# Cross-attention on one core: the last 26 keys as a fifth block of 32 instead of a transposition by TensorE

## The reference

```python
q = _split_heads(hidden_states @ Wq.T, H)
k = _split_heads(text @ Wk.T, H)
v = _split_heads(text @ Wv.T, H)
out_text = _merge_heads(_attend(q, k, v, sm_scale))
k_ip = _split_heads(ip @ Wk_ip.T, H)
v_ip = _split_heads(ip @ Wv_ip.T, H)
out_ip = _merge_heads(_attend(q, k_ip, v_ip, sm_scale))
out = out_text + IP_SCALE * out_ip
out = out @ Wo.T + bo
return out + residual
```

## Time and profile before

| | |
|---|---|
| median of 3 runs | 549.65 us (548.14 to 549.90) |
| the profiled execution | 547.71 us, span 545.7 us |
| TensorE busy | 517.2 us, 95% of the span |
| TensorE weight loads | 451.1 us, 83% |
| VectorE busy | 400.9 us, 73% |
| ScalarE busy | 386.0 us, 71% |
| GpSimd busy | 309.9 us, 57% |
| DMA | 130.13 MB, 78.8% of 16 engines' span, mean 238 GB/s |
| granted clock of TensorE, mean | 0.987 |

### The profile page before, as it was taken

The page is one execution under the profiler, slowest core; times in us unless marked ns, Lnnn a source line. Parts: engine busy times, 40 slices in busy tenths (PEclk is TensorE's granted clock), DMA queues, the critical chain, the costliest instruction groups (busy, mean ns, idle before and its releaser), DMA issues.

```text
span 545.7 us, 15177 instructions
## 1 busy us (share of the span) xinstructions
PE 517.2 (95%) x4994; PEld 451.1 (83%) x4994; DVE 400.9 (73%) x655; ACT 386.0 (71%) x1714; POOL 309.9 (57%) x343
## 2 busy tenths in 40 slices
PE   8999777899999999999999999999999999999897
PEld 8999666688887888888887888887888888888685
DVE  0024598988787888878887878887888878888822
ACT  0145578787877787878877887877887878877720
POOL 1032536566665848666747666666748566756530
PEclk9999878999999999999999999999999999999999
DMA  8992166877978787979788878888798979878772
GB/s 287 412 385 118 40 198 193 260 222 201 308 216 280 215 264 237 276 212 281 228 259 228 260 231 252 262 240 259 215 272 230 272 218 276 233 229 229 231 220 88
DMA packets 87005, 130.13 MB, mean 238 GB/s; under 512 B 9792, under 2 KB 71872, under 8 KB 86720
## 3 DMA queue, kind: packets, MB, share of 16 engines
q1 hardware_dynamic: 86976, 129.75, 78.8%
HBM read 77.29 MB, written 52.43 MB: 238 GB/s over the span
## 4 chain that ended last, share of the span: by engine, by line
PE 50%; issue 12%; POOL 11%; DMA 9%; DVE 7%; SPq 5%; ACT 5%; POOLq 0%; DVEq 0%; ACTq 0%
PE q_ps L633 13%; PE x_ps L633 13%; DMA p_main<-bounce_d 8%; POOL probs L343 6%; PE s_ps L658 5%; PE pv_ps L682 5%; PE pv_ps L679 4%; SPq L288 4%; PE s_ps L771 3%; ACT probs L406 3%; POOL res L368 2%; DVE row_neg L534 2%; PE pv_ps L771 2%; DVE turned L553 2%; POOL rest L349 2%
## 5 line engine op out<-in xcount | busy, mean ns | idle before, releaser
L343 POOL TENSOR_TENSOR probs<-probs,row_inv 128x616 f32<-128x616 f32 (+1 forms) x160 | 165.4, 1054 | 165.9 <-DVE row_inv L565 165.9
L406 ACT ACTIVATE probs<-s_ps,row_neg 128x77 f32<-128x77 f32 x640 | 197.9, 338 | 63.5 <-DVE row_neg L534 63.4
L534 DVE TENSOR_REDUCE row_neg<-s_ps 128x8 f32<-128x616 f32 x160 | 120.4, 794 | 34.4 <-PE s_ps L658 34.0
L406 ACT ACTIVATION_READ_ACCUMULATOR probs<-s_ps,row_neg 128x1 f32 x640 | 139.7, 218 | 0.0
L553 DVE STREAM_TRANSPOSE turned<-probs 128x512 f32<-128x512 f32 x160 | 103.9, 686 | 2.9 <-POOL probs L343 2.7
L560 DVE TENSOR_REDUCE row_sum<-probs 128x8 f32<-128x616 f32 x80 | 63.6, 795 | 42.6 <-ACT probs L413 42.6
L633 PE MATMUL q_ps<-x_hi,wq_hi 128*128 128x256 f32 x400 | 90.0, 324 | 0.0
L633 PE MATMUL x_ps<-attn_hi,wo_hi 128*128 128x256 f32 x375 | 75.4, 299 | 1.1 <-ACT y L431 1.1
L633 PE MATMUL q_ps<-x_hi,wq_lo 128*128 128x256 f32 x400 | 74.7, 285 | 0.0
L633 PE MATMUL q_ps<-x_lo,wq_hi 128*128 128x256 f32 x400 | 74.4, 284 | 0.0
L334 POOL TENSOR_TENSOR x_lo<-x_raw,x_hi 128x1280 fp32r<-128x1280 f32 x16 | 48.8, 3049 | 44.1 <-ACT x_hi L424 44.1
(11 more groups left out here) (72 smaller groups left out, 756.4 us busy)
## 6 DMA issues: line engine op xcount, KB each, us to landing
bounce_d<-turned SPq DMA_DIRECT2D x80, 512.0 KB, 3.0
p_main<-bounce_d SPq DMA_DIRECT2D x320, 128.0 KB, 3.5
x_raw<-x_in SPq DMA_DIRECT2D x16, 640.0 KB, 6.4
res<-x_in SPq DMA_DIRECT2D x75, 128.0 KB, 3.3
y_out<-res SPq DMA_DIRECT2D x75, 128.0 KB, 3.0
stage<-wk_in SPq DMA_DIRECT2D x6, 640.0 KB, 8.3
stage<-wv_in SPq DMA_DIRECT2D x6, 640.0 KB, 11.1
wq_raw<-wq_in SPq DMA_DIRECT2D x1, 1600.0 KB, 10.3
```

The costliest lines, as they stand in the source:

```text
L343: nc.gpsimd.tensor_tensor(rows[:, :, keys], rows[:, :, keys], row_inv[:, u.slot, :, br].unsqueeze(2) .broadcast_to([P, GROUP * SUB, size]) ...
L406: done = nc.scalar.activation(rows[:, cols], s_ps[:, j, cols], ACT.Exp, bias=row_neg[:, j, i:i + 1], accum_out=row_sum[:, j, i:i + 1])
L534: nc.vector.tensor_reduce(row_neg[:, heads_of(half)], by_row(s_ps[:, heads_of(half), 0:SUB * BLK]), AXIS.X, ALU.max, negate=True).then_inc ...
```

## The change

The last 26 keys take the way of the others, as a fifth block of 32. The probabilities get 64 zero columns at the end of each place, so that VectorE's second transposition may read past the last head's keys; it now does three blocks (the six rows beyond the 26 carry other heads' numbers and aren't loaded). The write to DRAM grows by a quarter, a fifth load brings 26 partitions into `p_last`, whose other rows stay zero, and TensorE does four more column products over it. `normalise_rest`, `turn_rest`, `keep_rest`, `head_rows` and `rest_of_values` go. The values of the last keys are transposed straight from `v_chan`, which is zero behind them.

Beside this `p_main` goes from five places to two and with `p_last` is protected by `pv_ready`, now one semaphore a place; SyncE issues three of a unit's loads before the next unit's write and two behind it; ScalarE does the direct head 0, then `exp`, then the direct head 1; and one residual load of the end moves behind the last loads. The warm-up has 5 + 2 matmuls instead of 7, the last two of which count up `pv_ready`.

```diff
-            def load_turned(u):
-
-                wait(sp, bounced[u.slot], u.uses_of_slot(DMA))
-                for b in range(BLOCKS):
-                    sp.dma_start(p_main[rows_of(b), u.g].rearrange("k a j s n -> k a (j s n)"),
-                                 bounce_d[u.g, :, b].rearrange("(a k) n -> k a n", a=BLOCKS)
-                                 ).then_inc(p_loaded[u.g], DMA)
+            def load_turned(u, blocks):
+
+                uses = u.uses_of_slot(DMA)
+                if blocks[0] == 0:
+                    if u.fixed and u.number() == 0:
+                        sp.wait_ge(padded, 3)
+                    wait(sp, pv_ready[u.slot], uses)
+                    wait(sp, bounced[u.slot], uses)
+                for b in blocks:
+                    to = p_main[rows_of(b), u.slot] if b < BLOCKS else p_last[0:REST, u.slot]
+                    sp.dma_start(to.rearrange("k a j s n -> k a (j s n)"),
+                                 bounce_d[u.g, :, b].rearrange("(a k) n -> k a n", a=BLOCKS)[0:min(D, BLK - b * D)]
+                                 ).then_inc(p_loaded[u.slot], DMA)
 
             def emit(u):
...
+                if u.plus(-2).exists():
+                    load_turned(u.plus(-2), range(0, 3))
                 if u.plus(-1).exists():
                     bounce(u.plus(-1))
                 if u.plus(-2).exists():
-                    load_turned(u.plus(-2))
+                    load_turned(u.plus(-2), range(3, KEY_BLOCKS))
...
-            load_residual(LAST.plus(-1))
             bounce(final)
             for u in (final.plus(-1), final):
-                load_turned(u)
+                load_turned(u, range(KEY_BLOCKS))
+            load_residual(LAST.plus(-1))
...
-                for br, keys in enumerate((slice(0, KEYS), slice(KEYS, MAIN))):
+                for br, keys in enumerate((slice(0, KEYS), slice(KEYS, BLK))):
...
+            def exps(u):
+                exp_direct(u, range(0, 1))
+                exp(u)
+                exp_direct(u, range(1, PAIR))
...
-                size = BLOCKS // BRANCHES
-                keys = slice(part * size * D, (part + 1) * size * D)
-                nc.vector.transpose(turned[:, u.slot, part * size:(part + 1) * size],
-                                    probs[:, u.slot].rearrange("p j s n -> p (j s) n")[:, :, keys]
-                                    .rearrange("p q (b k) -> p b q k", k=D)).then_inc(p_turned, 1)
+                first, end = ((0, 2), (2, KEY_BLOCKS))[part]
+
+                rows = probs[:, u.slot, first * D:first * D + ROWS].rearrange("p (q n) -> p q n", n=BLK)
+                nc.vector.transpose(turned[:, u.slot, first:end],
+                                    rows[:, :, 0:(end - first) * D].rearrange("p q (b k) -> p b q k", k=D)
+                                    ).then_inc(p_turned, 1)
...
-                wait(pe, p_loaded[u.g], u.tile(BLOCKS * DMA, BLOCKS * DMA))
-                wait(pe, rest_kept, u.number(1, 1))
+                wait(pe, p_loaded[u.slot], u.uses_of_slot(KEY_BLOCKS * DMA))
                 wait(pe, attn_lo_done, u.number())
-                for j in range(GROUP):
-                    nc.tensor.matmul(pv_ps[rows_of(j), 0:N].rearrange("c (s a k) -> c a s k", s=SUB, a=BLOCKS),
-                                     v[:, u.g, u.batch, rows_of(j)], p_main[:, u.g, :, j],
-                                     start=True, stop=False, skip_group_check=True)
-                nc.tensor.matmul(pv_ps[:, 0:N], v[:, u.g, BATCHES + u.batch, :], p_rest[:, u.g], start=False, stop=True,
-                                 skip_group_check=True).then_inc(pv_ready, 1)
+                for part, p in enumerate((p_main, p_last)):
+                    for j in range(GROUP):
+                        done = nc.tensor.matmul(pv_ps[rows_of(j), 0:N].rearrange("c (s a k) -> c a s k", s=SUB, a=BLOCKS),
+                                                v[:, u.g, part * BATCHES + u.batch, rows_of(j)], p[:, u.slot, :, j],
+                                                start=(part == 0), stop=(part == 1), skip_group_check=True)
+                done.then_inc(pv_ready[u.slot], DMA)
```

More of the change, by code:

```diff
@@ L344, in normalise @@
                                             .broadcast_to([P, GROUP * SUB, size]), ALU.mult).then_inc(p_done, 1)
-            def normalise_rest(u):
-                shape = [P, SUB, GROUP, REST]
-                wait(pool, rest_turned, u.number())
-                nc.gpsimd.tensor_tensor(rest[:, :, :, 0:REST], probs[:, u.slot, :, :, MAIN:].rearrange("p j s n -> p s j n"),
-                                        row_inv[:, u.slot, :, 1].rearrange("p (j s) -> p s j", s=SUB).unsqueeze(3)
-                                        .broadcast_to(shape), ALU.mult).then_inc(rest_done, 1)
-            def rest_of_values(g):
-                if g == 0:
-                    for n in range(2):
-                        pool.wait_ge(v_kept[n], BRANCHES)
-                    pool.wait_ge(head_rows_done, 1)
-                shape = [P, BATCHES, GROUP, REST]
-                nc.gpsimd.tensor_tensor(v_rest[:, g, :, :, 0:REST], v_chan[:, g].rearrange("p b r n -> p b (r n)")[:, :, MAIN:]
-                                        .unsqueeze(2).broadcast_to(shape),
-                                        head_rows[:].unsqueeze(1).unsqueeze(3).broadcast_to(shape), ALU.mult
-                                        ).then_inc(v_rest_done, 1)
             def add_residual(c):
@@ L381, in _ @@
             split_x(Unit(0, GROUPS))
-            for g in range(GROUPS):
-                rest_of_values(g)
             emit.engine = pool
@@ L397, in keep_q, with exp_direct @@
                 nc.scalar.activation(q[:, u.slot, :], q_ps[:, 0:N], ACT.Copy).then_inc(q_done, 1)
-            def exp_direct(u):
-                wait(act, max_done, u.number(2, 1))
-                for j in range(PAIR):
-                    rows = probs[:, u.slot, j].rearrange("p s n -> p (s n)")
+            def exp_direct(u, heads):
+                if heads[0] == 0:
+                    wait(act, max_done, u.number(2, 1))
+                for j in heads:
+                    rows = probs_of(u)[:, j].rearrange("p s n -> p (s n)")
                     for i in range(SUB * BRANCHES):
@@ L407, in exp_direct @@
                                                     bias=row_neg[:, j, i:i + 1], accum_out=row_sum[:, j, i:i + 1])
-                done.then_inc(direct_done, 1)
+                if heads[-1] == PAIR - 1:
+                    done.then_inc(direct_done, 1)
             def exp(u):
                 wait(act, sub_done, u.number(1, 1))
-                rows = probs[:, u.slot, heads_of(1)]
+                rows = probs_of(u)[:, heads_of(1)]
                 nc.scalar.activation(rows, rows, ACT.Exp).then_inc(exp_done, 1)
-            def keep_rest(u):
-                wait(act, rest_turned, u.number(1, 1))
-                nc.scalar.activation(p_rest[:, u.g], rest_ps[:, 0:N], ACT.Copy).then_inc(rest_kept, 1)
+            def exps(u):
+                exp_direct(u, range(0, 1))
+                exp(u)
+                exp_direct(u, range(1, PAIR))
             def split_x(u):
@@ L433, in attn_high @@
             def attn_high(u):
-                wait(act, pv_ready, u.number(1, 1))
+                wait(act, pv_ready[u.slot], u.plus(2).uses_of_slot(DMA))
                 nc.scalar.activation(attn_hi[:, u.batch, u.g, :], pv_ps[:, 0:N], ACT.Copy).then_inc(attn_hi_done, 1)
@@ L440, in emit @@
                 chunk = u.plus(-OUT_LAG)
-                if u.plus(-2).exists():
-                    keep_rest(u.plus(-2))
-                exp_direct(u)
-                exp(u)
+                exps(u)
                 if u.plus(-VALUE_LAG).exists():
@@ L505, in _ @@
             final = LAST.plus(GROUPS - 1)
-            keep_rest(final.plus(-1))
             add_bias(LAST.plus(-4))
@@ L511, in _ @@
             add_bias(LAST.plus(-2))
-            keep_rest(final)
             attn_high(final.plus(-1))
@@ L754, in emit @@
                     project_q(u.plus(Q_AHEAD))
-                turn_rest(u.plus(-1))
                 if chunk.exists():
@@ L777, in turn_v @@
             def turn_v(g):
-                pe.wait_ge(v_rest_done, g + 1)
+                if g == 0:
+                    pe.wait_ge(padded, 1)
+                    for n in range(2):
+                        pe.wait_ge(v_kept[n], BRANCHES)
                 if g >= 3:
@@ L792, in _ @@
             for _ in range(WARM_UP):
-                nc.tensor.matmul(x_ps[:, 0:P], ident[:], ident[:], start=True, stop=True)
+                done = nc.tensor.matmul(x_ps[:, 0:P], ident[:], ident[:], start=True, stop=True)
+            for n in range(2):
+                done = nc.tensor.matmul(x_ps[:, 0:P], ident[:], ident[:], start=True, stop=True)
+                done.then_inc(pv_ready[n], DMA)
             for br in range(BRANCHES):
@@ L819, in _ @@
             pe.wait_ge(v_done, GROUPS)
-            turn_rest(first)
```

74 lines of the change are left out of this document (29 added, 45 removed).

## The result

| | before | changed |
|---|---|---|
| median | 548.89 us (546.71 to 549.90, 4 runs) | 569.59 us (565.57 to 572.63, 4 runs) |
| ratio, 95% interval | | **1.0378** [1.0304, 1.0452] |
| profiled execution, span | 547.71, 545.7 | 568.92, 567.0 |
| TensorE's clock, mean | 0.987 | 0.958 |
| units 0 to 12 (start of scores to start of scores), profiled | 78.2 us | 83.3 us |

The forecast was 541 us in 525 to 561. The change is slower by 20.7 us, outside the range. In the profiled executions it comes from three places: 65 x 0.176 = 11.4 us in the loop, 5.1 us in the opening, and some 4 us behind unit 77. All ratios leave out an execution over 1.5% above the fastest of its kernel, which in `e1_order` is one of four and in `e9_x_pieces_no_split` four of ten.

The account below looks back on a forecast made before the run. TensorE was taken as full in four units of five, DMA holding it up in the fifth. 65 units at 5.70 instead of 5.83 us give -8.5 us: 539.2 profiled, 541 us as median, range 525 to 561.

Parts of the forecast that it names:

- TensorE's unit: TensorE in the loop: without `turn_rest` and the `p_rest` product, with four column products over `p_last`, 5.73 becomes 5.55 us.
- VectorE and ScalarE: Loop: fifth transposed block adds 0.32 us, sums stop waiting for the exponential; compute engines together allow 5.50 to 5.55 us.
- Transfers, "I take 5.70": DMA in the loop: 1640 KB a unit instead of 1408, at 295 GB/s for a full share, 5.70 us a unit.
- It costs nothing while this holds: SyncE's loads with `p_main` at two places: the older product is done at 1.9 us, the write landed at about 2.3.
- rival (3): SyncE's circle of landing, three loads, next write: 5.1 us, 9.4 with a late landing; 5.9 us a unit, 554 us; chance 0.06.
- (2): Rival: DMA engines hold only 280 GB/s, 6.0 us a unit, 561 us, TensorE waiting in most units; chance 0.25.
- The loads are used two units later, which should absorb half: In the SyncE circle rival: 0.8 us a unit from late landings, half absorbed, leaving 5.9 us a unit.
- Rival (1): Transfers keep up and the compute engines bound the loop: 5.50 us a unit, 528 us; chance 0.20.
- Both ends at nothing, 1 us either way: Ahead of the loop and at the end: removed and added work costed at nothing, 1 us either way.

Follow-up runs that it names:

- e1_order: The changed kernel with SyncE's old order, a unit's write ahead of all five loads of the older unit: 585.46 us, ratio to before 1.071.
- e9_x_pieces_no_split: The changed kernel with x_raw in two places, loaded in four pieces, and ScalarE's direct heads both ahead of the exponential again: 547.63 us, ratio to before 0.9973.
- f1: The changed kernel with x_raw in two places, loaded in pieces of 256, 256 and 128 KB in units g = 0, 1, 2: 552.27 us, ratio to before 1.0109.
- e4: The changed kernel without the loads of x_raw in the loop, the first two tiles used for all: 532.11 us, ratio to before 0.9763.
- g1: The changed kernel with x_raw in pieces of 256, 256 and 128 KB, GpSimd's first normalisation waiting for VectorE's first three wo_lo: 551.03 us, ratio to before 1.0098.
- e3_no_last_load: The changed kernel without the fifth load, the last 26 keys left out of the output: 558.00 us, ratio to before 1.0192.

## Why the prediction was wrong

- **TensorE's unit, 5.55 us (5.24 to 5.57):** right. `p_last` took 0.55 us as forecast; unstalled units last 5.41 to 5.47 us.
- **VectorE and ScalarE:** right in mechanism. The transposition grew by 0.27 us (forecast 0.32), the row sums wait no more, `attn_lo` ends 5.94 us behind the scores (192.70 - 186.76; forecast 6.2). That the split would be worth something because of this was not borne out: the transposition waits for its write anyway.
- **Transfers, "I take 5.70":** this step failed. It took an average rate for the whole. The wait for the write's landing it put at nothing, from a landing of 3.0 us ("It costs nothing while this holds"), and in rival (3) the circle at 5.1 us, with 3.0 + 0.3. The landing took 4.55 us on average, and the circle 6.03, which is the pace. Two parts can be told apart. With x_raw spread, the pace is 5.78 to 5.80 us, at 290 GB/s where 295 were assumed: 0.09 us above 5.70, 6 us in all. The other part is the burst. x_raw puts 640 KB in front of one write of 640 KB, the loads can't be issued until that write has landed (up to 7.7 us in this loop), and the following turns of the circle, at 5.3 to 5.7 us, have no slack to catch up. Before, that cost 0.5 us once in five; the same event now cost 2.4. This is 6.01 - 5.79 = 0.22 us a unit, 14 us.
- **The clock:** no term of the sum. Five waits of 1.73 to 3.17 us in the changed kernel's loop were followed by stretches at 1.2 GHz, which in the unit at 175.96 doubled the loss (2.6 us and then 2.7). Of the 14 us of the burst up to 10 are of this kind.
- **Rivals:** (2) had the right pace (6.0) for the wrong reason: it wanted a share above 0.93 and waits in most units; the changed kernel has 0.89 and waits in one of five. f1 is what (2) describes in kind, at 5.80. (3), with 0.06, had the right place, the late landing behind x_raw, and its signature, over 5.85 us at a share below 0.93. The write followed the write by 8.05 us, where it had 9.4. Its mechanism is the one that the trace shows, in nearly every unit and not only behind x_raw; what it lacked is the size, a landing of 3.3 us instead of 3.9 to 4.2 in the ordinary units, and the clock. It doesn't follow that the old order would have been better: e1, which loosens the circle, is 16 us slower. "The loads are used two units later, which should absorb half" held neither before nor now. Rival (1)'s 5.5 us a unit was met by e4 alone, and there too by the circle.
- **"Both ends at nothing, 1 us either way":** wrong by 5.1 us at the start and about 4 at the end. Removing `rest_of_values` was costed as a saving of GpSimd's time; it was also what kept GpSimd's first normalisation away from VectorE's `wo_lo`, which is 2.1 of the 5.1 us; the rest is open. The end was not tried by itself. There the product with the values waits up to 1.90 us for its loads, and the granted clock behind unit 77 is 0.94 against 1.00 before.

The sum against the profiled execution: forecast 539.2, measured 568.92. (6.008 - 5.70) x 65 = 20.0 us, 5.1 and 4.2 at the ends: 29.3 of 29.7 us.

## What to carry to other kernels

Where a queue carries one large transfer among many small ones, add up the bytes between one large transfer and the moment its followers are needed, besides the bytes of the period: here a share of 0.84 in a five-unit window hid a place that had no slack left. Before adding bytes to such a queue, spread the large one over the period; that alone gave 1.0% in the old kernel and 16 to 18 us in the new one. Where a queue's own order makes a circle (landing, loads, next write), compare it with the unit by the landing times of a busy queue, and look in the new profile whether a write leaves when its data is ready. And when work is removed from an engine that waits anyway, ask what now starts earlier, and beside what.

## What the runs showed that I had not expected

- GpSimd's and VectorE's elementwise work on float32 in SBUF slowed each other when they ran together: from f1 to g1, with a single wait as the difference, three of VectorE's went from 6.54 to 4.47 us and two of GpSimd's from 3.58 to 2.42. Of the three only the second and third changed, from 1.85 to 0.81 us each; the first stands beside GpSimd's x_lo and takes 3.0 us in both.
- The price of a stall is not its length. In the changed kernel's loop waits of 1.65 us and less left the clock alone, and one of 2.57 us cost 5.3. It isn't a plain rule: in e1_order a wait of 2.83 us was followed by no lower clock, in e3_no_last_load one of 1.94 neither.
- The last of the five loads takes 0.94 us to issue where the others take 0.43, with 26 rows as with 32 (0.97). Neither its rows nor its being the last is the reason. In `e1_order`, from 120 to 480 us, it is the last too and takes 0.41:

```profile
L293 SPq DMA_DIRECT2D p_last<-bounce_d x57: 406/407/806, 123.3 to 476.2; - x57
```

  There the second load is the slow one, with a median of 0.99 us. In all sixteen kernels the slow issue is the second transfer behind the write to DRAM, whatever it is: 0.78 to 1.04 us for a load, and 0.70 instead of 0.36 for the residual that stands there in `e3_no_last_load`. Why is open.
